# The second token group's end of a mixture-of-experts FFN, moved into the attention that follows, and a bias added by VectorE

## The reference

```python
x = layernorm(x + gather_conv(x))          # first mixer
xn = layernorm(x) * ln_g + ln_b
abel = gelu(xn @ abel_w + abel_b)          # dense branch
wdense = softmax of the two largest of (xn @ gate_w + gate_b)
moe = sum over e of wdense[e] * (gelu(xn @ w1[e] + b1[e]) @ w2[e] + b2[e])
nonabel = moe @ rot                        # rot: product of three expm(gens[i])
g = sigmoid(concat(abel, nonabel) @ mix_w + mix_b)
x = layernorm(x + (x + abel * (1 - g) + nonabel * g))
x = layernorm(x + attention(x))            # 16 heads of 8 channels
x = layernorm(x + second_ffn(x))           # 8 experts, two per token
```

## Time and profile before

| | |
|---|---|
| median of 3 runs (lowest, highest) | 770.09 us (767.79, 770.35) |
| the profiled execution | 769.04 us, of which 767.2 us from the first to the last instruction |
| TensorE busy | 530.9 us (69%) |
| VectorE busy | 532.9 us (69%) |
| ScalarE busy | 413.9 us (54%) |
| GpSimd busy | 210.0 us (27%) |
| the attention's first product to the end of its last stretch | 441.96 to 637.5 us, 195.54 us |

### The profile page before, as it was taken

The page is one execution under the profiler, slowest core; times in us unless marked ns, Lnnn a source line. Parts: engine busy times, 40 slices in busy tenths (PEclk is TensorE's granted clock), DMA queues, the critical chain, the costliest instruction groups (busy, mean ns, idle before and its releaser), DMA issues. The chain is left out here.

```text
span 767.2 us, 14477 instructions
## 1 busy us (share of the span) xinstructions
PE 530.9 (69%) x5186; PEld 439.8 (57%) x5186; DVE 532.9 (69%) x1210; ACT 413.9 (54%) x909; POOL 210.0 (27%) x195
## 2 busy tenths in 40 slices
PE   5457766764675679999862267888868976898720
PEld 3346655654565679889861244455545545898720
DVE  2998999899999356466652558788887606656634
ACT  5485677678784345457752334677765343333320
POOL 1031113113116726205307160000000160345243
PEclk9567887687686969999995567999988558999975
DMA  8344454844455223113201040000000011233222
GB/s 252 86 134 139 127 154 114 241 124 127 145 160 157 79 77 91 46 55 107 68 25 51 4 165 0 2 1 2 1 2 2 6 49 43 76 114 112 63 76 58
DMA packets 98891, 63.96 MB, mean 83 GB/s; under 512 B 57218, under 2 KB 89476, under 8 KB 98692
## 3 DMA queue, kind: packets, MB, share of 16 engines
q1 hardware_dynamic: 94564, 54.12, 24.7%
q0 software_dynamic: 4256, 8.92, 3.8%
HBM read 40.33 MB, written 22.68 MB: 82 GB/s over the span
## 5 line engine op out<-in xcount | busy, mean ns | idle before, releaser
L1879 DVE TENSOR_REDUCE mx<-s_ps 128x2 f32<-128x512 f32 x128 | 82.5, 687 | 30.0 <-PE s_ps L1633 29.9
L1816 ACT ACTIVATE pt<-st_ps 128x512 f32<-128x512 f32 x128 | 69.8, 600 | 39.2 <-PE st_ps L1643 38.4
L344 POOL DMA_INDIRECT xd<-xs_all,r_posA x32 | 39.0, 1220 | 160.7 <-DVE r_posA L328 151.6
L1278 ACT ACTIVATE hid<-up,wblk 128x128 f32<-128x128 f32 x184 | 52.8, 374 | 46.3 <-PE up L1177 46.3
L638 ACT ACTIVATE tap<-cst_s,par 128x328 f32<-128x328 f32 x128 | 72.6, 661 | 3.8 <-DVE par L1003 3.8
L645 ACT ACTIVATE rest<-rest,par 128x264 f32<-128x264 f32 x128 | 53.9, 506 | 32.0 <-DVE rest L950 32.0
L626 POOL TENSOR_TENSOR kst<-kst 128x504 f32<-128x504 f32 x16 | 16.4, 1028 | 185.4 <-DVE kst L877 185.4
L1633 PE MATMUL s_ps<-kf,qf 32*128 32x256 f32 x256 | 35.9, 359 | 30.1 <-DVE mx L1879 26.4
L1377 DVE COPY wblk<-wslab 128x1156 f32 x46 | 37.0, 811 | 22.9 <-issue 13.4
L809 PE MATMUL yps<-AT,xn 128*32 128x64 f32 x1024 | 29.0, 300 | 34.0 <-ACT cfS L657 34.0
L1177 PE MATMUL up<-xsT,wblk 128*128 128x128 f32 x368 | 52.2, 288 | 0.0
(11 more groups left out here) (364 smaller groups left out, 1373.8 us busy)
## 6 DMA issues: line engine op xcount, KB each, us to landing
kd<-kst SPq DMA_DIRECT2D x16, 512.0 KB, 2.9
xc<-in_x_coarse SPq DMA_DIRECT2D x16, 512.0 KB, 4.4
yd<-eos SPq DMA_DIRECT2D x44, 128.0 KB, 1.9
xsb<-xd SPq DMA_DIRECT2D x20, 256.0 KB, 3.6
wslab<-in_w SPq DMA_DIRECT2D x8, 578.0 KB
dW<-kd SPq DMA_DIRECT2D x16, 256.0 KB, 3.3
wslab<-in_w SPq DMA_DIRECT2D x1, 3072.0 KB, 9.9
xd<-zero_t SPq DMA_DIRECT2D x2, 1472.0 KB, 11.1
```

The costliest lines, as they stand in the source:

```text
L344: nc.gpsimd.indirect_dma_start(out=rows, out_offset=bass.IndirectOffsetOnAxis(ap=R.pos[:, t, k:k + 1], axis=0), in_=x[:, R.first + t, :], ...
L1278: nc.scalar.activation(hid[j % 2][:, k, :], up_ps[j % 2][:, k * P:(k + 1) * P], ACT.Gelu, bias=wblk[j % 4][:, 2 * DF + k:2 * DF + k + 1]). ...
L1816: nc.scalar.activation(pt[h % 8][:].rearrange("p t q -> p (t q)"), st_ps[k][:], ACT.Exp, scale=SCALE)\
L1879: nc.vector.tensor_reduce(mx[:, :, h:h + 1], s_ps[k][:].rearrange("p (t k) -> p t k", t=2), AX, ALU.max).then_inc(s_used, 1)
```

## The change

The dense branch's bias is no longer a matmul: `abr` now holds the bias on all partitions, VectorE adds it while it copies the sums out of `aux` (`abel_added`), and ScalarE's GELU works in place in SBUF. The steps of part 1 are moved forward in the loop, by two to four blocks at the start, so that its row mixing and its rows out stand inside the loop too. GpSimd's splitting of parts 0 and 1 goes ahead of its wait for group B's stores, and group B's gather leaves this stage.

Group B's end runs in the attention stage. GpSimd gathers the rows after its clearing, weighs and adds them itself (class `Tail`: eight multiplications and one addition per part), adds the constant row in three pieces, normalises the rows of parts 2 and 3, and splits their columns. TensorE, ScalarE and VectorE get the other steps between the rounds' own steps, in rounds 1 to 4, with PSUM banks of the attention. Some tiles and semaphores live longer; `add_row` reuses `zero_t`.

```diff
+class Tail:
+    def mixture(self, nc, pool, k, first_done):
...
+        for t in range(k * TC, (k + 1) * TC):
+            for h in range(2):
+                last = nc.gpsimd.tensor_scalar(self.got[:, t, h, :], self.got[:, t, h, :], R.pr[:, t, h:h + 1], None, ALU.mult)
+        last.then_inc(first_done, 1)
+        pool.wait_ge(first_done, k + 1)
+        last = nc.gpsimd.tensor_tensor(self.got[:, own, 0, :], self.got[:, own, 0, :], self.got[:, own, 1, :], ALU.add)
...
             route_gather(nc, first, yd[0])
+            for q in range(2):
+                columns_split(q)
             for i in range(len(PAIRS) - 3, len(PAIRS)):
                 pool.wait_ge(eos_out[i % 3], 16 * (i // 3 + 1))
-            route_gather(nc, second, yd[1])
-            for q in range(2):
-                columns_split(q)
...
                 for t in range(TC):
-                    nc.tensor.matmul(aux[:, t * P:(t + 1) * P], R.cols[...], aw[:], start=True, stop=False)
-                    last = nc.tensor.matmul(aux[:, t * P:(t + 1) * P], ones_row[:], abr[:], start=False, stop=True)
+                    last = nc.tensor.matmul(aux[:, t * P:(t + 1) * P], R.cols[...], aw[:], start=True, stop=True)
...
-                if j in (34, 40):
-                    mixture_turned((j - 34) // 6)
-                if j in (36, 43):
-                    rotated((j - 36) // 7)
+                if j in (34, 38):
+                    mixture_turned((j - 34) // 4)
+                if j in (36, 41):
+                    rotated((j - 36) // 5)
                 if j == 42:
                     turned_back(0)
             turned_back(1)
-            mixture_turned(2)
-            rotated(2)
-            mixture_turned(3)
-            turned_back(2)
-            rotated(3)
-            turned_back(3)
...
-                nc.scalar.activation(flat2(abel[:, q * TC:(q + 1) * TC, :]), aux[:], ACT.Gelu).then_inc(ab_done, 1)
+                nc.scalar.activation(flat2(abel[q]), flat2(abel[q]), ACT.Gelu).then_inc(ab_done, 1)
...
-                if j in (32, 38):
-                    weighted_first((j - 32) // 6)
+                if j in (32, 36):
+                    weighted_first((j - 32) // 4)
...
+            def abel_added(q):
+                v.wait_ge(ab_ready, q + 1)
+                nc.vector.tensor_tensor(abel[q], aux[:].rearrange("p (t c) -> p t c", t=TC), bc(abr[:], 1, TC), ALU.add)\
+                    .then_inc(ab_added, 1)
...
+                if j in (10, 12, 14, 16):
+                    abel_added((j - 10) // 2)
+                if j in (13, 16, 19, 22):
+                    residual((j - 13) // 3)
+                if j in (14, 17, 20, 23):
+                    own_share((j - 14) // 3)
+                if j in (33, 37):
+                    mixture((j - 33) // 4)
+                if j in (37, 42):
+                    mixed((j - 37) // 5)
+                if j in (39, 44):
+                    rows_mixed((j - 39) // 5)
+                if j in (41, 46):
+                    rows_out((j - 41) // 5)
...
+            tail.gather(nc, yd[1])
+            for k in range(2):
+                tail.mixture(nc, pool, k, mixed_first).then_inc(moe_set, 1)
...
+                pool.wait_ge(ro_set, k + 1)
+                for t in range(TC):
+                    last = nc.gpsimd.tensor_scalar(rows[:, t, :], dn[u][:, t, :], mv2[:, t, 0:1], ro[:, u, t:t + 1],
+                                                   ALU.subtract, ALU.mult)
+                last.then_inc(xs_ready, 1)
...
                 scores(i, 2)
                 values(i - 1, 0)
+                if i in (1, 2):
+                    mixture_turned(i - 1)
+                if i == 3:
+                    rotated(1, (x_ps[0], x_ps[2]))
+                if i in (2, 4):
+                    turned_back(i // 2 - 1)
...
+                    if i == 3:
+                        pe.wait_ge(dn_done, 4)
                     by_token(i - 2, 0, 0)
...
                 scores(i, 4)
+                if i == 1:
+                    rotated(0, (x_ps[0], x_ps[1]))
...
                 powers(i - 1, 2)
+                if i in (1, 2):
+                    mixture_copied(i - 1)
+                if i in (2, 4):
+                    columns_out(i // 2 - 1)
                 powers(i - 1, 3)
+                if i == 3:
+                    mix_share(1)
...
                 powers(i - 1, 5)
+                if i == 1:
+                    mix_share(0)
...
                 powers(i - 1, 6)
+                if i == 3:
+                    root(1)
...
                 powers(i - 1, 7)
+                if i == 1:
+                    root(0)
...
                 largest(i, 0)
+                if i == 2:
+                    inverse(0)
...
                 largest(i, 3)
+                if i == 3:
+                    mixed(1, (x_ps[0], x_ps[2]))
...
                 largest(i, 4)
+                if i == 1:
+                    mixed(0, (x_ps[0], x_ps[1]))
...
                 largest(i, 5)
+                if i == 3:
+                    rows_mixed(1)
...
                 add_maxima(i, 0, 0)
+                if i == 1:
+                    rows_mixed(0)
                 largest(i, 7)
+                if i == 3:
+                    inverse(1)
```

227 lines of the change are left out of this document (146 added, 81 removed).

## The result

| | median | lowest to highest | ratio to before (95% interval) |
|---|---|---|---|
| before | 768.94 us | 766.76 to 770.35 | |
| changed | 735.46 us | 731.37 to 741.0 | 0.957 (0.950 to 0.964) |

A forecast was written before the change was run, and what follows sets the result against it. TensorE bounds the first FFN's loop, a serial chain across engines the second group's end, VectorE nearly the attention. 769.04 - 8.5 + 0.2 - 36.0 + 10.0 = 734.7, so 735 us, range 727 to 749.

The forecast's parts named there:

- Part 1: First FFN's dense branch: bias on VectorE saves TensorE 9.4 us, less 0.9 for late VectorE: -8.5 us.
- 32.5 us of VectorE: First FFN loop, blocks 10 to 23: VectorE's counted need, against 29.5 us for TensorE.
- Part 2: End of first FFN's loop: first group's second part brought forward; delays and returned waits net +0.2 us.
- ScalarE's wait for the gathers: Loop after block 36: ScalarE waits 3.1 us in order, making following products about 2.1 us late.
- Part 3: Tail between last expert product and attention: attention starts at 405.95 instead of 441.96, -36.0 us.
- the 0.5 us that the step between the stages takes: Entry to the attention: its start follows GpSimd's end at 405.4 by 0.5 us.
- Part 4: Attention rounds 1 to 4: the moved second-group work costs +10.0 us, bounds +4 to +20.
- GpSimd is too slow for the mixture: Attention: GpSimd's sixteen scalings delay everything behind them; 786 us at 5 us per scaling, chance 0.04.
- its own formula: Attention: second mixture late by 16 T - 29 us, T being us per GpSimd scaling; gain gone from T = 3.9.
- the attention gives most back: Attention: moved steps paid in series, 30.6 us in place of 10; 755 us, chance 0.11.
- the table loads: Attention's ScalarE: a switch costs 1.28 us, not the skill's 2.66; tanh loads, 5.1 us, only in the upper bound.
- the second rival's cases: Whole kernel time: given as beginning at 750 us, the reason for ending the forecast range at 749.

The follow-up runs named there:

- the repeated run: The changed kernel measured again unchanged, on one chip with the three combined-edit kernels: 735.36 us, ratio 0.961.
- pieces: Changed kernel with each of the attention's two row mixings cut in two, gate and sums earlier in the round: 733.69 us, ratio 0.955.
- late row: Changed kernel with GpSimd's addition of the constant row to parts 2 and 3 put off behind a later VectorE step: 731.5 us, ratio 0.953.
- fill: Changed kernel with 22 unused matmuls on TensorE in its waits for the two row mixings: 733.69 us, ratio 0.955.
- the second joint one: Changed kernel with the last column split on VectorE, GpSimd's row addition put off and 22 unused matmuls in TensorE's waits: 724.87 us, ratio 0.948.
- all: Changed kernel with VectorE's last split, row mixings cut in two, row addition put off, 8 unused matmuls, second part's mixing before fourth maxima: 723.12 us, ratio 0.944.
- the delayed run: Changed kernel with sixteen more GpSimd scalings by 1.0 between the gathers and the first mixture: 741.76 us, ratio 0.968.
- the run with the split: Changed kernel with the last split of the first FFN's columns on VectorE instead of GpSimd: 737.02 us, ratio 0.958.

## Why the prediction was right, and where its terms were off

The time (735 forecast, 735.46 measured) and the mechanism hold: the old tail went, and the attention took a third of it back. That the sum came out within 1 us is partly luck: of the four terms two were off by 3 us each and in opposite senses, a third was right only as a sum, and 3.2 us of the difference between the two traces are stretches of the lower clock in the loop that the trace of before has and that of after lacks.

- **Part 1**, -8.5: -9.7 in the trace to block 32. The bias's own part of it is 8.1, by the run that puts the matmul back; the other 1.6 is a dip of the clock in the trace of before (0.96 granted from 310 to 350 us), which that run and the changed kernel lack. The 0.9 us that the term charged, for expert products held up by a late VectorE, didn't come: no expert product waits there. In its place the dense parts wait 0.8 us for VectorE's sums, which the prediction didn't name, so the agreement is chance. (Its 32.5 us of VectorE are 33.0 with the 2.8 us of additions and the four times 2.4 that it names.)
- **Part 2**, +0.2: -2.6 at the loop's end, of which 1.64 is the lower clock in the trace of before and 0.5 to 1.4 the bias (37.84 to 37.31 without the new order, 36.68 to 35.27 with it). The new order itself gave 0.4 us (37.31 to 36.91, both with the lower clock) or cost 0.5 (36.2 to 36.68 with the matmul; 36.2 is an estimate, 37.84 - 1.64). So the +0.2 was about right, but not its terms. The step that failed is ScalarE's wait for the gathers, 3.1 us with 2.1 us of late products: it was 1.56 us (1.96 in the repeated run), and TensorE waited 0.35. The view counts the 2.8 us to landing from the start of the issue, so the prediction counted its 0.95 us twice (the gather of 372.6 landed at 375.34, not 376.35), and the last gather landed 0.7 us earlier as the blocks count.
- **Part 3**, -36.0: -33.1. Copy and split took what the rows said. The step that failed is "the 0.5 us that the step between the stages takes": it took 2.97, with GpSimd now the last engine to end, so the attention's first product came 9.7 us behind the last expert product and not 6 to 7. Some 0.5 us more is the row mixing, held up by GpSimd's split of the first part.
- **Part 4**, +10.0: +11.4, but not as counted. Up to the start of round 5 the attention lost 16.1 us, rounds 5 to 7 lost 0.8 more, and the last two gave 5.5 back. By steps against the same steps before: up to the start of round 2 2.7 net (3.2 counted for round 1), of which the step with the first row mixing is 2.5; the turning behind the second part's mixing 1.9 (2.05), the second row mixing 2.0 (2.7), the splits and negations of rounds 2 and 4 1.5 and 1.1 (0.2 each), and, counted nowhere, three dips of the clock of 1.6 us, 4.7 in all. The last step of round 3 is 1.9 us longer, and there two causes lie over each other. The changed kernel has a dip of the clock in it, and without the root it falls by 0.5. But in five runs (pieces, late row, fill, the second joint one, all) the clock is 1.00 throughout that step, and it still takes 3.83 to 4.57 us (4.37 in the changed kernel, 2.45 before), with TensorE waiting 1.31 to 1.71 us for ScalarE's exponentials, which stand behind the load after the root. So the root with its two loads costs 1.4 us or more there (1.1 counted), the dip without the root as much (3.84 us), and to take away either one alone gains at most 0.5; no run takes away both. In the last two rounds the trace of before has a clock of 0.50 from 605 to 625 us, that of after 0.81 and 0.70 in the two 10 us stretches from 576, so the products there are faster; that too I had not counted. From the last scores on, the twelve traces with the moved end take 25.4 to 26.0 us and the two without 31.0; why the clock differs there stays open.

In the table of stretches of before, those last two rounds:

```profile
605.20:615.20 10.00, 8.82 (x61) 4.65 (x60) 5.33 (x19) 3.62 (x8) 3.52 (x4) 0.50 0.06 21
615.20:625.20 10.00, 8.82 (x58) 4.99 (x60) 1.00 (x4) 4.86 (x10) 7.57 (x9) 0.50 0.15 52
```

and in that of after:

```profile
576.00:586.00 10.00, 8.73 (x84) 4.78 (x84) 5.33 (x19) 5.10 (x10) 3.55 (x4) 0.81 0.06 21
586.00:596.00 10.00, 7.45 (x59) 3.96 (x60) 1.00 (x4) 6.29 (x12) 7.56 (x9) 0.70 0.16 53
```

**The rivals.** That GpSimd is too slow for the mixture was excluded by its rows, and the runs show how far off it was: 0.58 us a scaling in the changed kernel, and a margin of 4.85 us, which the delayed run confirms. (By its own formula it would eat the gain from T = 4.0 on, not 3.9.) That the attention gives most back is nearer than the chance of 0.11 says for its mechanism (16.1 us lost in the first five rounds, 4.7 of them by the three dips of the clock), though not for its time. On the table loads both halves came out as the trace had it: the tanh needs none (0.22 us at 438.64), and a switch costs its load of 1.28 us. The Trainium skill's "ScalarE: Activation LUTs" says the first in its table of sets, and the trace agrees. The 2.66 us a switch of the Trainium skill's "ScalarE: Activation LUTs", section "What ACT_TABLE_LOAD costs", don't appear: the root starts 0.02 us behind the end of its load. (The sentence of the prediction that lets "the second rival's cases" begin at 750 meant the first rival.)

## What to carry to other kernels

Price a step that is moved onto another engine not only by its own duration but by what it runs beside: here a GpSimd operation of 1.3 us made a VectorE operation of 0.19 us last 1.21, and the loop waited for it. When the last work of a stage changes its engine, look up what the step into the next stage costs behind that engine, because it need not be the old figure. And when an alternating loop must take in more work, keep TensorE busy in its longest wait and let GpSimd's work not run beside VectorE's: the same change was worth 33 us as made and 43 to 45 with these edits. Before a cost of 1 or 2 us is given to a cause, look at the granted clock of both traces, and at a second trace of the same kernel.

## What the runs showed of the hardware

- VectorE's operations that read SBUF ended when GpSimd's two-input operations beside them ended, or up to 0.15 us later: 0.96 and 1.21 us for 0.17 and 0.19, 0.89 for 0.16 (387.06 in the run with the split), and the first of four mixing operations, which made 2.03 of 1.14. The maxima out of PSUM at 455.14, beside GpSimd's cast, took their usual 1.29. The Trainium skill's "SBUF — State Buffer", section "Who interferes with whom", states an exclusive lock between the two engines, for VectorE's operations with two inputs in SBUF and for some with one; all rows here agree.
- A stage began 2.90 to 2.97 us after GpSimd's last work in the changed kernel, whose VectorE and ScalarE ended 1.7 us and more ahead, and 0.3 to 0.5 us after VectorE or ScalarE in the kernel before, where GpSimd had ended 6.7 us and more ahead of them.
- The granted clock fell behind waits of TensorE of 1.45 and 2.87 us in a loop whose clock had been 1.00 throughout those rounds. With the wait of 2.87 filled with matmuls whose results nobody uses, it stayed at 1.00 behind it, in three runs of three. Behind the other place it stayed at 1.00 after a wait of 0.43 us, but also after 1.45 and 1.47, and fell after one of 0.42: what decides there is open.
- The same loop code took 35.27 us in six traces and 36.90 or 36.91 in five with a stretch of the lower clock, so two traces of one kernel can differ by 1.6 us in such a place.
